# Another order of a period's steps on four engines of a fused attention and expert kernel

## The reference

```python
# cross-attention: 16 heads of 128, 257 context rows of width 128 per sequence
q = rmsnorm((ln(x) @ Wq).reshape(B, Sq, H, D), gq)
k = rmsnorm((ctx @ Wk).reshape(B, Skv, H, D), gk)
x = x + softmax(q @ k.T / sqrt(D)) @ (ctx @ Wv) @ Wo
# causal self-attention: 16 query heads, 4 key heads of 16, ternary weights, RMS norms, rotary
x = x + ternary(rms_norm(attn(rope(rms(q)), rope(rms(k)), v)), w_proj)
# mixture of 8 experts, top 1, 256 slots each, and one shared expert
x = x + gate * keep * expert_out[slot] + (silu(xt @ sw1) * (xt @ sw3)) @ sw2
```

## Time and profile before

| | us |
|---|---|
| median of 3 runs | 1754.23 (1750.4 to 1756.08) |
| profiled execution, whole | 1746.76 |
| its span | 1744.5 |
| PE busy | 1508.3 (86%) |
| DVE busy | 1024.8 (59%) |
| ACT busy | 800.3 (46%) |
| POOL busy | 374.3 (21%) |

### The profile page before, as it was taken

How to read it: one execution, slowest core, us unless ns; L and a number is a source line. 1 busy time by engine, 2 the same in 40 slices (tenths; PEclk the granted TensorE clock), 3 DMA queues, 4 the chain that set the end, 5 groups by cost and what they waited for, 6 DMA issues and landing times.

```text
span 1744.5 us, 31551 instructions
## 1 busy us (share of the span) xinstructions
PE 1508.3 (86%) x9114; PEld 1007.1 (58%) x9114; DVE 1024.8 (59%) x3844; ACT 800.3 (46%) x3319; POOL 374.3 (21%) x890
## 2 busy tenths in 40 slices
PE   5779899999999898999989998989899998975772
PEld 2536656475646566665647564656656565645662
DVE  6746666665657575666657565657566665723112
ACT  4455554554555454445545454545454554521110
POOL 2131312222130313122221212131312222110003
PEclk9989999999899999999999989999999999975897
DMA  8000000000000000000000000000000000100444
GB/s 345 6 16 13 26 9 21 16 9 22 12 25 12 22 12 25 12 22 13 15 22 9 22 12 25 12 22 12 24 9 22 15 9 24 54 6 0 131 153 124
DMA packets 40861, 59.46 MB, mean 34 GB/s; under 512 B 4918, under 2 KB 35777, under 8 KB 39744
## 3 DMA queue, kind: packets, MB, share of 16 engines
q1 hardware_dynamic: 36528, 50.37, 9.0%
q0 software_dynamic: 2064, 6.14, 1.1%
q10 hardware_dynamic: 2176, 2.10, 0.3%
HBM read 48.26 MB, written 10.49 MB: 34 GB/s over the span
## 4 chain that ended last, share of the span: by engine, by line
PE 42%; issue 32%; POOL 9%; ACT 9%; DVE 5%; DMA 3%; POOLq 1%; SPq 0%; DVEq 0%; ACTq 0%
PE AB L573 19%; PE Eb L573 8%; ACT AB L911 5%; PE Db L573 4%; PE C L573 3%; ACT px L980 2%; PE C L695 2%; DMA ctxn<-expert_rows 2%; PE AB L771 2%; PE C L712 2%; POOL c_lo L1078 2%; POOL rkx L1104 2%; POOL prob L1113 2%; POOL pjunk L1072 1%; POOL rstd L1089 1%
## 5 line engine op out<-in xcount | busy, mean ns | idle before, releaser
L911 ACT ACTIVATE AB<-AB 128x128 f32<-128x128 f32 (+1 forms) x1160 | 303.1, 261 | 261.5 <-PE AB L573 261.5
L1220 DVE BATCH_NORM_STATS2 kst<-AB 128x6 f32<-128x256 f32 x512 | 181.8, 416 | 148.3 <-PE AB L573 114.5
L1072 POOL TENSOR_TENSOR pjunk<-pjunk 128x1 f32<-128x1 f32 x208 | 40.7, 196 | 976.0 <-DVE sinv L1376 625.4
L573 PE MATMUL AB<-wk_hi,c_hi 128*128 128x512 f16 x512 | 203.1, 397 | 42.5 <-ACT AB L911 22.4
L911 ACT ACTIVATION_READ_ACCUMULATOR AB<-AB 128x1 f32 (+1 forms) x1160 | 215.4, 186 | 0.0
L573 PE MATMUL AB<-wk_lo,c_hi 128*128 128x512 f16 x512 | 201.7, 394 | 0.0
L573 PE MATMUL AB<-wk_hi,c_lo 128*128 128x512 f16 x512 | 200.3, 391 | 0.0
L970 ACT ACTIVATE prob<-prob,nbias,rq 128x257 f32<-128x257 f32 x256 | 150.8, 593 | 87.1 <-DVE nbias L1371 86.7
L573 PE MATMUL AB<-ctxT,qpT 128*128 128x257 f32 x512 | 136.0, 412 | 18.4 <-ACT AB L911 18.4
L573 PE MATMUL Eb<-pT,ctxn 128*128 128x512 f32 x256 | 127.7, 622 | 9.6 <-DVE base L1517 7.7
L573 PEld LDWEIGHTS AB<-wk_hi,c_hi 128*128 128x128 f16 x512 | 51.9, 101 | 126.2 <-issue 34.9
(11 more groups left out here) (237 smaller groups left out, 3085.8 us busy)
## 6 DMA issues: line engine op xcount, KB each, us to landing
ctxT<-in_ctxT SPq DMA_DIRECT2D x64, 128.5 KB, 2.1
ctxn<-in_ctxn SPq DMA_DIRECT2D x64, 128.0 KB, 2.1
wq_hi<-in_w SPq DMA_DIRECT2D x4, 768.0 KB, 5.2
wq_lo<-in_w SPq DMA_DIRECT2D x4, 768.0 KB, 5.9
expert_rows<-base POOLq DMA_DIRECT2D x1, 2048.0 KB, 16.2
xin<-in_x SPq DMA_DIRECT2D x16, 128.0 KB, 2.2
prob<-in_wqT SPq DMA_DIRECT2D x1, 2048.0 KB, 18.7
xres<-in_x SPq DMA_DIRECT2D x16, 128.0 KB, 2.0
```

What stands on the lines that cost most here:

```text
L573: return pe.matmul(out, lhsT, rhs, start=start, stop=stop)
L911: ins = nc.scalar.activation(k, k, ACT.Square, accum_out=sums[0:m, h:h + 1])
L1072: own.mark(pool.tensor_tensor(pjunk[:, 0:1], pjunk[:, 1:2], pjunk[:, 1:2], ALU.mult))
L1220: ins = V.bn_stats(stats[:, 0, n], AB[0:m, 2 + n // 2, 2 * D * (n % 2):2 * D * (n % 2 + 1)])
```

## The change

Only the four lists of the table for the loop are written anew. Every engine has the same steps; the start's table, the waits of each step, the buffers and SP's list stay. Words moved in the lists move whole blocks of instructions:

```diff
 ORDER = {
-    "PE": """K0 K1 X K2 pt3 K3 o3 Q f K4 rk0 xt1 K5 qkv QP K6 qk s0 sc rk1 K7 s1 pt pt0 pv s2 yt pr rk2 o0
+    "PE": """K0 K1 pt3 X K2 o3 K3 f Q xt1 K4 rk0 K5 qkv QP K6 qk s0 rk1 sc K7 s1 pt pt0 pv s2 yt pr pt1 o0 xt2
-    "DVE": """K0 X K1 K2 dp3 XL K3 KN0 do3 Q RQ f K4 K5 qkv K6 s0 sc K7 i0 s1 pt KN1 pv dp0 i1 pr ln2 s2 dp1
+    "DVE": """X K0 K1 dp3 XL K2 do3 K3 f KN0 Q K4 RQ K5 qkv K6 s0 sc i0 K7 s1 pt KN1 i1 pv dp0 pr ln2 dp1 do0 s2
...
-    "POOL": """h0 n3 h1 X h2 r0 r1 ln1 h3 n0 r2 y n1 ln2 r3 n2 scat""".split(),
+    "POOL": """h0 h2 h3 h1 X n3 ln1 r0 r1 n0 n1 y ln2 r2 r3 n2 scat""".split(),
 }
```

More of the change, by code:

```diff
@@ L147 @@
 ORDER = {
-    "PE": """K0 K1 X K2 pt3 K3 o3 Q f K4 rk0 xt1 K5 qkv QP K6 qk s0 sc rk1 K7 s1 pt pt0 pv s2 yt pr rk2 o0
-              pt1 xt2 lg up pos o1 rk3 s3 pt2 dn o2""".split(),
-    "ACT": """K0 K1 K2 tl3 X K3 oh3 Q K4 xt1 K5 qkv rk0 QP K6 qk e0 rk1 K7 sc pt tl0 e1 yt rk2 tl1 xt2 oh0 e2
-              lg up oh1 rk3 tl2 e3 oh2""".split(),
-    "DVE": """K0 X K1 K2 dp3 XL K3 KN0 do3 Q RQ f K4 K5 qkv K6 s0 sc K7 i0 s1 pt KN1 pv dp0 i1 pr ln2 s2 dp1
-              do0 lg i2 pos up do1 dp2 dn s3 i3 do2""".split(),
-    "POOL": """h0 n3 h1 X h2 r0 r1 ln1 h3 n0 r2 y n1 ln2 r3 n2 scat""".split(),
+    "PE": """K0 K1 pt3 X K2 o3 K3 f Q xt1 K4 rk0 K5 qkv QP K6 qk s0 rk1 sc K7 s1 pt pt0 pv s2 yt pr pt1 o0 xt2
+              rk2 lg up o1 pos rk3 dn pt2 s3 o2""".split(),
+    "ACT": """K0 K1 X tl3 K2 oh3 K3 Q K4 xt1 K5 qkv rk0 QP K6 qk e0 rk1 K7 sc pt e1 tl0 yt tl1 oh0 xt2 rk2 up e2
+              oh1 rk3 lg tl2 e3 oh2""".split(),
+    "DVE": """X K0 K1 dp3 XL K2 do3 K3 f KN0 Q K4 RQ K5 qkv K6 s0 sc i0 K7 s1 pt KN1 i1 pv dp0 pr ln2 dp1 do0 s2
+              lg up i2 do1 pos dn dp2 s3 i3 do2""".split(),
+    "POOL": """h0 h2 h3 h1 X n3 ln1 r0 r1 n0 n1 y ln2 r2 r3 n2 scat""".split(),
 }
```

## The result

| | before | after |
|---|---|---|
| median | 1752.32 (1745.46 to 1756.08, 4 runs) | 1799.56 (1798.03 to 1803.67, 4 runs) |
| ratio, 95% interval | | 1.0278 (1.024 to 1.0316) |
| profiled execution | 1746.76 | 1803.67 |
| its span | 1744.5 | 1801.5 |
| mean granted clock | 0.937 | 0.913 |

Slower by 47 us. The time lies inside the range of eight in ten (1763 to 1810), 14 us above the forecast and 0.6 above the upper end of the forecast's own range. A run more than 1.5% above the fastest of its kernel is left out of the ratios; that concerns one of e7's ten runs and seven of e9's, the profiled one of each among them, so their mean period is not given. The lower part of the table already says that it didn't come about as forecast: PE is busy 33 us longer with the same 9114 matmuls, and the clock went down.

What follows compares the result with a forecast made beforehand. PE's list was the path, its work plus waits. At full clock +2.65 us, less 0.5 for the clock, gave 2.15 for each of 14 periods; with the ends 1779, plus 7.5 to the median: 1786 us, eight in ten 1763 to 1810.

Steps and rivals of the forecast that it cites:

- the forecast's own range: Time expected if the main forecast of 1786 us holds: 1774 to 1799 us, given a chance of 0.57.
- the clock: Whole period: fewer stretches at PE's lower clock level, -0.5 us a period, bounds -3.0 to +1.95.
- Part A: From o2 to the start of Q or f: K1's second half later, X's wait gone, +1.25 us a period.
- The gap at the jump: DVE's 2.44 us gap at each loop jump back stays, whatever operation stands first.
- Rival 2: DVE's 2.44 us gap belongs to the first operation, so X runs inside it: 1756 us, no change; chance 0.07.
- Part B: From the start of Q or f to s0: DVE becomes the chain, +1.8 us a period.
- The three new waits: PE waits inside K4 (1.0), in QP (1.6) and for heads (1.15): 3.75 us in place of 2.0.
- F + 7.7: F is the end of f on PE; 7.7 us later DVE was to end Q's statistics.
- Part C: From s0 to o2: new waits at K7, up and dn, old ones gone at xt2, lg and o2; -0.4 us.
- dn's 0.35: In the late part, dn waits 0.35 us for do1, as e2 stands behind up and ahead of oh1 on ACT.
- rival 1: One more slow stretch behind K1's wait of about 3 us: 1820 us, or 1803 if only in some periods; chance 0.15.
- the forecast's full-clock sum: Waits added over the three parts of a period, 1.25 + 1.8 - 0.4 = 2.65 us for each with a jump.

Runs made afterwards that it cites:

- e7: Kernel before with the changed order from s0 on for PE, ACT and DVE, POOL's list as before; 1741.13 us, ratio 0.9957.
- e9: Changed kernel with K0 ahead of X on DVE, n3 ahead of X on POOL, the old middle, r0 and r1 ahead of ln1; 1733.81 us, ratio 0.9864.
- e2: Kernel before with X ahead of K0 on DVE, nothing else moved; 1763.22 us, ratio 1.0124.
- e11: Changed kernel with one swap undone, sc ahead of rk1 on PE; 1753.73 us, ratio 1.0034.
- e5: Changed kernel with K0 ahead of X on DVE and n3 ahead of X on POOL; 1732.58 us, ratio 0.9936.
- e10: e9 with sc ahead of rk1 on PE; 1709.59 us, ratio 0.9795.
- e8: e7 with sc ahead of rk1 on PE, as before the change; 1722.39 us, ratio 0.9874.
- e1: Changed kernel with K0 ahead of X on DVE again, POOL's list left as changed; 1771.5 us, ratio 1.0152.
- e3: Changed kernel with the middle of PE and DVE as before, POOL's list left as changed; 1822.64 us, ratio 1.0423.
- e4: Changed kernel with KN0 ahead of f on DVE; 1774.58 us, ratio 1.0185.

## Why the prediction was right, and where it was wrong

The sign and the range were right. The size came out 14 us higher, and the sum behind it was wrong in one term that outweighs the others, the clock.

- **Part A, X ahead of K0: right.** Forecast +2.05 for K1 and -0.8 for X. e2 shows 1.30 for the two together; 18.89 in e11 against 16.9 in e5 is 2.0 for K0's place, with n3 moved on POOL as well. K1's idle was to be 2.9 and is 2.61. The rest of the head's change was a gain of 1.0, of which the prediction saw 0.8.
- **The gap at the jump: right.** Rival 2 is refuted by the first of the waits after: another operation stands first on DVE, and 14 gaps of 33.4 us in all stand ahead of it, where they were 33.7. By the Trainium skill (Runtime: NRT & Kernel Launch, Instruction fetch mechanics) such a gap goes with the taken branch; this trace agrees, with 2.4 us on DVE. ACT, whose list jumps too, shows no such gap in either profile, and no run says why.
- **Part B: the mechanism right, the term too big.** The three new waits are where they were forecast, with idles of 0.56, 1.10 and 1.06. From start to start, the form of the prediction, they are 0.72, 1.26 and 1.22 where it had 1.0, 1.6 and 1.15: 3.2 in place of 3.75, against 2.0 before. So +1.2, not +1.8. DVE isn't quite back to back, as the prediction's last paragraph asked: it waits 1.56 for PE ahead of K4's second statistics, a wait that the prediction's own sum has (from F + 7.7 to the end of K4's second half). e9 adds what the prediction missed: f ahead of Q covers ACT's squares of K3, worth 1.3, so undoing part B brings nothing at full clock.
- **Part C: too pessimistic.** rk1 ahead of sc costs 0.65, not 0.9 (10.13 against 9.47 in e11). up waits 0.72 for ACT's copy, as forecast; dn's 0.35 didn't come. C is -1.0, not -0.4. At full clock the change costs 1.25 a period, half of the 2.65.
- **The clock: the step that failed.** Forecast -0.5 a period, measured +2.8. Two things were wrong in it. The slow stretch in K1 came in every period, behind a wait longer than any of the old ones: rival 1, which had 0.15. It is worth 1.55. And the argument that o0 between pt1 and xt2 breaks up the narrow work, and so spares a slow stretch, was wrong: one came at up in every period, and a double one at pv and s2. By the prediction's own condition (a share between 0.95 and 0.97) the forecast failed: the share is 0.93. Rival 1 gives 1820 with the forecast's full-clock sum; with the measured one, 1.4 x 14 less, it gives 1800. By the Trainium skill (TensorE: Matmul & The Clock Gate, HAM oscillation) idle gaps between bursts of matmuls bring the lower clock; K1 agrees, with a gap of 2.61 ahead of 3.4 us at the lower level. The stretches at pv and at up don't: no wait above 0.72 lies in the 15 us ahead of either, and the 0.72 is up's own, across the start of its stretch.

So the time fell into the range partly by luck, by two errors of opposite sign: the order's cost came out 1.4 a period lower than forecast and the clock's 3.3 higher. Of the 56 us between the profiled executions, 17 are waits at full clock and 39 are clock. The two errors make 26 us; only 14 of them show in the median, since the profiled executions lie further apart than the medians.

What isn't settled is why the late part of the changed kernel always falls into the pattern of pv and up, which makes 4.6 of its 6.1 us of clock. Orders with the same late part have the better one too (e5, from its eighth period on). With sc ahead of rk1 a double stretch at pv stands in one period of 14 in e11 and in one in e10, but still in four of e8, and no run shows which wait or which operation decides it. That the slow stretch in K1 follows the long wait is shown by both swaps, the one that brings the wait (e2) and the one that takes it away (e1, e5): with a wait of 2.5 to 3.1 a slow stretch begins between 1.0 us ahead of the wait's end and 1.3 us behind it in 14 of 14 periods (after, e3, e4), 13 of 14 (e2) and 12 of 14 (e11), without it, with 0.6 to 1.0 in its place, in none (before, e1, e5 to e10); where e1 has a long wait at pt3 instead, a slow stretch is there in 3 of 14. That the wait alone does it, and not also the transposes and products ahead of it at the end of the period, wasn't tried; three periods with the full wait have no slow stretch.

## What to carry to other kernels

Work a change of order out in two columns, the parts of a period at full clock and what the clock adds, and read each part from a stretch whose granted share is 1.00; a first iteration, or one odd period, often has it. The second column can't be had from waits: leave it a range as wide as the spread between periods of the same kernel, with the upper end not less likely than the lower. When one step of a list is moved, move its partners in the other engines' lists with it, or the undone half of a change shows up as a new wait (e1, e3 and e7), and test a reordering swap by swap, since good and bad swaps hide one another: here a kernel 2.1% faster lay inside a change that was 2.8% slower.

## What the runs showed that was not expected

- The same instructions take 92.1 or 95.5 us a period within one execution (e5), by where the lower clock falls, and the patterns hold for three and for seven periods. In after all 14 periods fall alike, and that kernel's four runs agree within 0.3%; the ten of e5 lie within 1.3% and those of e9 within 2.3%.
- An order's cost at full clock and its time can part widely: e1, e2 and after have 93.3, 92.9 and 92.9 us at full clock and take 96.7, 96.1 and 99.0.
- A microsecond at the lower level costs a little under half a microsecond here (6.1 for 13.6 in after, 3.3 for 7.3 in before): 1.55 for the stretch in K1, 1.3 for one at K7 and 1.7 for one at rk1 and K7, 3.0 for the double one at pv. That waits take up the rest is likely, but not shown.
